# Corner tiles in paired products, high parts on ScalarE, and a copy of the taps for the left and upper tiles

## The reference

```python
def _L0_conv_ref(x, kernel):            # x (128, 55, 55, 96), kernel (96, 5, 5), fp32
    ch = x.shape[-1]
    k = jnp.transpose(kernel, (1, 2, 0))[:, :, None, :]
    y = lax.conv_general_dilated(x, k, window_strides=(1, 1), padding='SAME',
                                 dimension_numbers=('NHWC', 'HWIO', 'NHWC'), feature_group_count=ch)
    return x + y
```

## Time and profile before

| | us |
|---|---|
| three runs | 820.22, 820.39 (median), 821.93 |
| the profiled execution | 820.37 |
| its span, first to last instruction | 818.6 |
| TensorE busy | 805.5 |
| VectorE, ScalarE, GpSimd busy | 690.1, 624.1, 525.6 |

### The profile page before, as it was taken

How to read it: one execution, slowest core, us unless ns; L and a number is a source line. 1 busy time by engine, 2 the same in 40 slices (tenths; PEclk the granted TensorE clock), 3 DMA queues, 4 the chain that set the end, 5 groups by cost and what they waited for, 6 DMA issues and landing times.

```text
span 818.6 us, 19135 instructions
## 1 busy us (share of the span) xinstructions
PE 805.5 (98%) x6912; PEld 805.4 (98%) x6912; DVE 690.1 (84%) x1828; ACT 624.1 (76%) x1442; POOL 525.6 (64%) x652
## 2 busy tenths in 40 slices
PE   5999999999999999999999999999999999999997
PEld 5999999999999999999999999999999999999997
DVE  6898888888888888888888888888888888888885
ACT  5777878787777778787777778787777777787775
POOL 7858566576665675756748566576565674756741
PEclk9999999999999999999999999999999999999999
DMA  9999999999999999999999999999999999999965
GB/s 357 426 426 408 375 381 363 383 368 385 368 370 389 364 381 376 375 381 364 378 377 379 386 368 370 377 376 378 382 361 382 372 386 376 368 376 376 381 261 229
DMA packets 28749, 304.43 MB, mean 372 GB/s; under 512 B 3184, under 2 KB 3312, under 8 KB 4208
## 3 DMA queue, kind: packets, MB, share of 16 engines
q1 hardware_dynamic: 28656, 303.22, 97.1%
HBM read 153.79 MB, written 149.42 MB: 370 GB/s over the span
## 4 chain that ended last, share of the span: by engine, by line
PE 98%; POOL 1%; DMA 0%; issue 0%; DVE 0%; ACT 0%; DVEq 0%
PE sums L380 33%; PE sums L383 33%; PE sums L382 33%; DMA first<-consts 0%; POOL matrix L263 0%; POOL spread L250 0%; POOL spare L238 0%; POOL taps L241 0%; POOL taps L236 0%; DVE y_out L333 0%; ACT y_out L292 0%; DVEq L132 0%
## 5 line engine op out<-in xcount | busy, mean ns | idle before, releaser
L380 PE MATMUL sums<-matrix,x_low 126*128 126x208 f32 (+5 forms) x2304 | 648.1, 281 | 8.3 <-POOL matrix L263 8.3
L383 PE MATMUL sums<-matrix,x_high 126*128 126x208 f32 (+5 forms) x2304 | 647.3, 281 | 0.0
L382 PE MATMUL sums<-matrix,x_high 126*128 126x208 f32 (+5 forms) x2304 | 646.3, 281 | 0.0
L292 ACT ACTIVATE y_out<-sums 128x270 f32<-128x270 f32 (+6 forms) x1152 | 443.4, 392 | 183.3 <-PE sums L383 179.5
L263 POOL TENSOR_TENSOR matrix<-spread,mask 127x300 fp32r<-127x300 f32 x384 | 338.5, 913 | 262.3 <-PE sums L383 262.1
L380 PEld LDWEIGHTS sums<-matrix,x_low 126*128 126x128 f32 (+1 forms) x2304 | 443.9, 193 | 8.2 <-POOL matrix L263 8.2
L383 PEld LDWEIGHTS sums<-matrix,x_high 126*128 126x128 f32 (+1 forms) x2304 | 444.3, 193 | 0.0
L382 PEld LDWEIGHTS sums<-matrix,x_high 126*128 126x128 f32 (+1 forms) x2304 | 444.2, 193 | 0.0
L333 DVE TENSOR_TENSOR y_out<-sums,y_out 128x120 f32<-128x120 f32 (+3 forms) x1344 | 295.5, 255 | 117.7 <-ACT y_out L292 113.8
L323 DVE TENSOR_TENSOR x_low<-x_in,x_high 128x768 fp32r<-128x768 f32 x384 | 379.8, 989 | 2.0 <-ACT x_high L285 2.0
L285 ACT ACTIVATE x_high<-x_in 128x768 fp32r<-128x768 f32 x288 | 239.8, 833 | 6.0 <-DMA x_in<-x 5.8
(11 more groups left out here) (4 smaller groups left out, 0.4 us busy)
## 6 DMA issues: line engine op xcount, KB each, us to landing
x_in<-x SPq DMA_DIRECT2D x95, 1536.0 KB, 9.9
y<-y_out SPq DMA_DIRECT2D x95, 1520.0 KB, 12.9
rest<-later SPq DMA_DIRECT2D x1, 2300.0 KB, 14.4
x_in<-x SPq DMA_DIRECT2D x4, 384.0 KB, 5.5
y<-y_out SPq DMA_DIRECT2D x1, 832.5 KB, 3.4
y<-y_out SPq DMA_DIRECT2D x1, 687.5 KB, 4.0
mask<-masks SPq DMA_DIRECT2D x1, 300.0 KB, 3.7
first<-consts SPq DMA_DIRECT2D x1, 125.0 KB, 2.1
```

What stands on the lines that cost most here:

```text
L292: act.activation(outputs(c, rows, cols), sums(c, t, rows, cols), ACT.Copy).then_inc(copied, 1)
L380: pe.matmul(target, low, turned[HIGH], start=tile is bank["tiles"][0], stop=False, skip_group_check=True)
L382: pe.matmul(target, high, turned[LOW], start=False, stop=False, skip_group_check=True)
L383: product = pe.matmul(target, high, turned[HIGH], start=False, stop=last, skip_group_check=True)
```

## The change

1. **Corner pairs.** In the four corner tiles (tile 0 of quarter 0, the fifth of quarter 1, the last of quarter 2, the second of quarter 3) the two products with `x_high` become one matmul. It streams the low and the high taps' slices, one behind the other (2 x 11 x 16 columns), and writes two places of the bank: the high product where it stood, the low one in 16 extra cells of each row. Banks with a corner so have rows of 46 cells. VectorE adds the low part to `y_out` in an add of its own of 11x16 cells.
2. **High parts.** `cast_high` is gone; ScalarE makes all four quarters' `x_high`, after banks 1, 3, 5 and 7; `x_low` stands after banks 4, 6, 7 and 9 instead of 4, 5, 7 and 9.
3. **Border tiles.** GpSimd copies, after the two parts of each kind's matrix, columns 2 to 17 of 14 of its rows into `edge`, where the 16 cells of a row lie without a gap. The tiles with `from_col` 2 read their taps there. TensorE's wait for a matrix now counts the copy too (`STEPS`).

```diff
+CORNERS = ((0, 0), (2, 0), (2, 1), (0, 1))
+SPAN = 2 * LONG + HALO
+EDGE = LONG + HALO
+EDGE_ROWS = SHORT + 2 * HALO + 1
+STEPS = 3 * KINDS
-HIGH_AFTER = (2, 5, 7)
-CAST_AFTER = 2
-LOW_AFTER = (4, 5, 7, 9)
+HIGH_AFTER = (1, 3, 5, 7)
+LOW_AFTER = (4, 6, 7, 9)
...
+            row, k = CORNERS[quarter]
+            corner = k if n == row else None
...
+                              deep=short[1] - short[0], pitch=SPAN + EDGE * (corner is not None)))
...
+        if bank["corner"] is not None:
+            cells_of_corner = bank["corner_cells"]
+            after = [n + 1 for n, e in enumerate(earlier) if meet(e, cells_of_corner)]
+            bank["adds"].append((cells_of_corner, after[-1] if after else 0, LOW))
+            earlier.append(cells_of_corner)
...
+        edge = [[sbuf(f"edge{i}_{k}", [P, 2, EDGE_ROWS, EDGE], F32R) for k in range(KINDS)] for i in range(SLOTS)]
...
+        def low_sums(c, t):
+            plane = plane_of(c, t)[:, :, SPAN:SPAN + EDGE]
+            return plane.rearrange("p x y -> p y x") if PLAN[t]["kind"] == TALL else plane
+
+        def both_sums(window, wide):
+
+            return bass.AP(tensor=window.tensor, offset=window.offset,
+                           ap=[window.ap[0], [SPAN - wide[0], 2], window.ap[1], window.ap[2]])
...
+                    pool.wait_ge(matrix_step, STEPS * c + 3 * kind + 2)
+                    pool.tensor_copy(
+                        edge[c % SLOTS][kind][0:whole, :, :, :],
+                        matrix[c % SLOTS][kind][0:whole, :, :].bitcast(F32).rearrange("p h (r q) -> p h r q", q=COLS)[
+                            :, :, 0:EDGE_ROWS, HALO:HALO + EDGE]).then_inc(matrix_step, 1)
...
-                dve.tensor_copy(x_high[c % SLOTS][:, cols], x_in[c % X_SLOTS][:, cols]).then_inc(cast_done, 1)
...
-                    dve.tensor_tensor(y, sums(c, t, rows, cols), y, ALU.add).then_inc(added, 1)
+                    terms = sums(c, t, rows, cols) if part == HIGH else low_sums(c, t)
+                    dve.tensor_tensor(y, terms, y, ALU.add).then_inc(added, 1)
...
-                            pe.wait_ge(matrix_step, 2 * KINDS * c + 2 * (kind + 1))
+                            pe.wait_ge(matrix_step, STEPS * c + 3 * (kind + 1))
...
+                        if tile["from_col"]:
+                            turned = edge[c % SLOTS][kind][0:pixels, :, cells, :]
+                        else:
+                            turned = matrix[c % SLOTS][kind][0:pixels, :, :].rearrange("p h (r q) -> p h r q", q=COLS)[
+                                :, :, cells, 0:wide[1] - wide[0]]
...
+                        if bank["corner"] is not None and tile is bank["tiles"][bank["corner"]]:
+                            product = pe.matmul(both_sums(target, wide), high, turned, start=False, stop=last,
+                                                skip_group_check=True)
```

More of the change, by code:

```diff
@@ L79, in banks_of_plane @@
                     from_row=short[0] - (v - HALO), from_col=a - (u - HALO)))
-            banks.append(dict(quarter=quarter, kind=kind, rows=rows, cols=cols, tiles=tiles,
-                              deep=short[1] - short[0], pitch=long[1] - long[0]))
+            row, k = CORNERS[quarter]
+            corner = k if n == row else None
+            banks.append(dict(quarter=quarter, kind=kind, rows=rows, cols=cols, tiles=tiles, corner=corner,
+                              deep=short[1] - short[0], pitch=SPAN + EDGE * (corner is not None)))
+            if corner is not None:
+                across_it = tuple(long[0] + w for w in tiles[corner]["wide"])
+                banks[-1]["corner_cells"] = (rows, across_it) if kind == FLAT else (across_it, cols)
     return banks
@@ L326, in add_seams @@
             def add_seams(c, t):
-                for n, ((rows, cols), after) in enumerate(PLAN[t]["adds"]):
+                for n, ((rows, cols), after, part) in enumerate(PLAN[t]["adds"]):
                     if n == 0:
@@ L375, in _ @@
                         high, low = x_high[c % SLOTS][0:pixels, images], x_low[c % SLOTS][0:pixels, images]
-                        turned = [matrix[c % SLOTS][kind][0:pixels, part, :].rearrange("p (r q) -> p r q", q=COLS)[
-                            :, tile["from_row"]:tile["from_row"] + deep,
-                            tile["from_col"]:tile["from_col"] + wide[1] - wide[0]] for part in (HIGH, LOW)]
+                        cells = slice(tile["from_row"], tile["from_row"] + deep)
+                        if tile["from_col"]:
[3 more added lines that the diff above has]
+                                :, :, cells, 0:wide[1] - wide[0]]
                         last = tile is bank["tiles"][-1]
-                        pe.matmul(target, low, turned[HIGH], start=tile is bank["tiles"][0], stop=False,
+                        pe.matmul(target, low, turned[:, HIGH], start=tile is bank["tiles"][0], stop=False,
                                   skip_group_check=True)
-                        pe.matmul(target, high, turned[LOW], start=False, stop=False, skip_group_check=True)
-                        product = pe.matmul(target, high, turned[HIGH], start=False, stop=last, skip_group_check=True)
+                        if bank["corner"] is not None and tile is bank["tiles"][bank["corner"]]:
+                            product = pe.matmul(both_sums(target, wide), high, turned, start=False, stop=last,
+                                                skip_group_check=True)
+                        else:
+                            pe.matmul(target, high, turned[:, LOW], start=False, stop=False, skip_group_check=True)
+                            product = pe.matmul(target, high, turned[:, HIGH], start=False, stop=last,
+                                                skip_group_check=True)
                     product.then_inc(sums_done, 1)
```

26 lines of the change are left out of this document (6 added, 20 removed).

## The result

The changed kernel takes 839.12 us in the median of four runs (838.68 to 840.10), the kernel before 820.52 beside it: a ratio of 1.0225, with an interval of 1.0207 to 1.0243. It is slower by 2.2 per cent, where 788.7 us were forecast, and lies outside the range of 780 to 806.

What follows compares the result with a forecast made beforehand. The prediction took TensorE to bound the kernel, its matmuls spaced by weight loads or rows. From 820.4 us it took 21.1 for corner pairs and 11.1 for border copies and added 0.5 at the start: 788.7 us, range 780 to 806.

Steps and rivals of the forecast that it cites:

- pairs: TensorE, four corner tiles a channel: one matmul of 0.169 us replaces two of 0.112 each, gaining 21.1 us.
- border copies: TensorE, six left and upper tiles: packed rows of 16 make matmuls faster, 0.116 us a channel, gaining 11.1 us.
- rival 4: Border tiles on TensorE: column offset is not why they are slow; two pairs cost 0.200 us, total 806; chance 0.06.
- GpSimd goes from 526 to 718 us: GpSimd's busy time with 192 new copies at 1.0 us each, in a span of some 787 us.
- near 702 to 710 us: VectorE's busy time after losing 88 us of casts and gaining 100 us of adds, below TensorE's new 780.
- a hold of 0.21 us for each new copy: GpSimd's new copies: held up by VectorE like the spread copies in the median, 560 against 347 ns.
- Rival 3: VectorE becomes late: copies hold x_low, adding 83 us, so VectorE reaches 793 and the kernel some 803; chance 0.06.
- The two new waits of low adds: VectorE: low adds wait for an earlier VectorE add, said to stand behind adds done in order anyway.
- Rival 1: GpSimd becomes the bound: passes TensorE at 1.28 us a copy, the old time at 1.44; chance 0.11.
- Rival 2: DMA holds the pace: a channel's 3.13 MB at 376 GB/s take 8.32 us, total 816; chance 0.07.
- ScalarE: ScalarE's busy time goes from 624 to 704 us by taking the first quarter's high part, 0.83 us a channel.
- The start: TensorE's first matmul, at 8.25 us before, comes 0.5 us later behind a copy; bounds -0.2 and +1.7.

Runs made afterwards that it cites:

- e5_act_edge: e1_reorder with the two border copies of a channel made by ScalarE instead of GpSimd; 786.99 us, ratio 0.9596 to the kernel before.
- e8_act_edge_no_pair: e6_act_edge_plain with the corner pairs undone, leaving of the change the border copies by ScalarE; 809.96 us, ratio 0.9868.
- e2_no_edge: The changed kernel without the border copies, so border tiles read the matrix at column 2 again; 805.89 us, ratio 0.9819.
- e4_reorder_no_edge: e1_reorder without the border copies, so border tiles read the matrix at column 2 again; 805.57 us, ratio 0.9817.
- e9_idle_copy: e5_act_edge with two more copies a channel on GpSimd, into a buffer that nobody reads; 826.72 us, ratio 1.0071.
- e7_half_low: e1_reorder with x_low computed for half of the columns, low parts of half of the tiles left out; 785.86 us, ratio 0.9573.
- e1_reorder: The changed kernel with the low adds of banks 0, 5 and 8 moved behind later seams and the first x_low one bank later; 832.23 us, ratio 1.0140.
- e3_no_pair: The changed kernel without corner pairs, keeping the GpSimd border copies and the high parts on ScalarE; 824.8 us, ratio 1.0052.
- e6_act_edge_plain: The changed kernel with the two border copies of a channel made by ScalarE, VectorE's order left as it is; 802.32 us, ratio 0.9772.

## Why the prediction was wrong

**What bounds the kernel, pairs, border copies: right.** TensorE bounded the kernel before, and its terms come out wherever the other engines let it run. The sum gave 788.7 us and 8.02 a channel; e5_act_edge takes 786.99 and 7.99. The copies alone were to gain 11.1 us less 0.5 at the start, and gain 10.6 (e8_act_edge_no_pair). The prediction's sum has a slip that hardly counts: three times 0.02 is 0.06, not 0.068. The pairs were to gain 21.1 and gain 23.0. Without the copies two of the four pairs read the matrix at column 2, and rival 4 had these at 0.200 instead of 0.169: 820.4 - 21.1 + 2 x 0.031 x 96 = 805.3, and e2_no_edge and e4_reorder_no_edge take 805.9 and 805.6. It shows in the timeline of the weight loads of a pair (L407, L423) and the two behind it, in e4_reorder_no_edge and in e5_act_edge (start us, us): the second and third are 0.20 apart where the pair reads from column 2, 0.16 where it reads the copy.

```profile
301.50 0.19 PEld L407 LDWEIGHTS sums<-matrix,x_high 126*128 126x128 f32 x1
301.61 0.19 PEld L404 LDWEIGHTS sums<-matrix,x_low 126*128 126x128 f32 x1
301.81 0.19 PEld L410 LDWEIGHTS sums<-matrix,x_high 126*128 126x128 f32 x1
```

```profile
300.73 0.19 PEld L423 LDWEIGHTS sums<-edge,x_high 126*128 126x128 f32 x1
300.85 0.19 PEld L420 LDWEIGHTS sums<-matrix,x_low 126*128 126x128 f32 x1
301.01 0.19 PEld L426 LDWEIGHTS sums<-matrix,x_high 126*128 126x128 f32 x1
```

By the median over the 96 channels of e4_reorder_no_edge, 0.31 us lie between the first and the third of these starts at the two corners that read column 2, and 0.28 at the two that read column 0. In e5_act_edge it is 0.28 at all four, and their places in the banks are the same. So the column offset is why those tiles were slow, and rival 4 falls.

**The step that failed: "GpSimd goes from 526 to 718 us ... still with idle time" and VectorE "near 702 to 710 us ... These edits cost nothing as long as that holds".** The copy's own price was about right (0.86 for 1.0). Left out was what the copy, and to a lesser part the new order, does to the instructions that stood there already. GpSimd came to 756: the 526 of before, copies of 165, matrices 66 longer, spread copies 19 longer (125 instead of 106), the splitting of the taps 16 shorter, and overlaps. VectorE came to 795, and the 82 us of `x_low` are nearly all of the miss: without them it stands at 713. Of these 82, 61 go with the copies, and of the matrices' 66, 20 (e2_no_edge). The prediction costed a hold of 0.21 us for each new copy and none for its partner. In the runs it falls on both sides: e9_idle_copy for VectorE by GpSimd's load, e7_half_low for GpSimd by VectorE's.

**Rival 3 had the mechanism and its price (83 us on `x_low`, VectorE at 793), with a chance of 0.06, and a time 36 us too low.** It was set aside because `x_low` stood at a median of 947 against a least of 939. That median was read wrongly as a sign that GpSimd hardly holds it. It says only that less than half were held: 93 of 384 took over 1.0 us, and the mean, 989, and the most, 1579, had already shown what a meeting costs. GpSimd then waited 262 us for TensorE; where the new copies take that waiting away (e9_idle_copy beside e5_act_edge), `x_low`'s median goes from 948 to 1218. That the 83 us came so near is partly luck: they were 0.43 for each of 192 copies, where 384 `x_low` grew by 0.21 each.

An estimate that fits the runs whose chain is GpSimd's or TensorE's: a channel needs on GpSimd, by the least or median durations, four matrices of 0.836, two copies of 0.57, two spreads of 0.356 and some 0.45 for the taps (0.58, 0.62 and 0.61 where nothing meets them, every fourth channel), 5.65 us; and on VectorE four `x_low` of 0.947, 3.79. Together 9.44 if they never overlap, over a channel of 8.0. The runs in which GpSimd sets the pace (e1_reorder, e3_no_pair, e9_idle_copy) go at 8.50, 8.40 and 8.45, about nine tenths of that sum. Without GpSimd's copies the sum is 8.30, with half of `x_low` 7.84; nine tenths of these lie under 8.0, and TensorE sets the pace in both. The factor is fitted, not explained; a part of it is that neighbours on one engine overlap, as the two matrices that take 1.61 and not 1.67 when nothing holds them.

The prediction had quoted the Trainium skill (SBUF — State Buffer, section "SBUF: two separate sides") for a lock that holds a VectorE instruction with two SBUF inputs and a GpSimd one that reads SBUF apart, either way round, and worked it out for the new copies alone. The runs bear the rule out in direction, on both engines; in size only roughly: beside an `x_low` of 0.96 the two matrices at the start were 0.73 late by the median of one matrix, and 0.80 by the 1.61 that two take together when nothing holds them. The same section says that ScalarE never waits there, and the copy on ScalarE agrees, 588 to 682 ns in all 192 of e5_act_edge against 562 to 1397 on GpSimd.

**"The two new waits of low adds ... stand behind adds that are done in order anyway": wrong.** They are in order, but an add that waits for the one before it loses their overlap: in the trace of the change an add that follows another at once and need not wait for it starts some 0.08 us before that one ends (median), and the four of a channel that must wait start 0.03 to 0.10 us after. That is 19 to 22 us of VectorE's busy time (e6_act_edge_plain against e5_act_edge, e2_no_edge against e4_reorder_no_edge, the change against e1_reorder). There are also three such new places in a channel and not two: the first seam add now waits for the low add of bank 0. The last step from rival 3's 803 to 839 lies in part in such losses: the page has 30.8 us of idle time before the adds, of which only 4.3 end with ScalarE; in e1_reorder it is 46.0 of 47.9. The adds in turn free the banks and `y_out` slots for which TensorE and ScalarE wait. How much of the 36 us is each was not parted, and with the waits gone GpSimd still holds the kernel at 832 (e1_reorder): rival 3 had left out that `x_low` holds GpSimd too.

**Rival 1** (GpSimd the bound) is what e1_reorder and e3_no_pair become, though with copies at 0.95 us, far under the 1.44 that it asked for: again because the matrices grew. **Rival 2** (DMA) falls as the bound: e5_act_edge moves 392 GB/s, as the forecast wanted. **ScalarE** was costed too high (704, measured 666). **The start**: the first matmul comes at 9.55, +1.3 instead of +0.5, inside its bounds.

## What to carry to other kernels

Work put on an engine with idle time can be paid for by work that stood there already, on that engine and on another. Before giving GpSimd a copy, add up the unheld time of GpSimd and of VectorE's instructions with two inputs in SBUF over one period. Here copies on GpSimd cost time where the sum was 9.44 us for a period of 8.0, and at 8.30, with the copies on ScalarE, they did not. A median near the least says only that less than half of the instructions were held, not that meeting is cheap; look at the mean and the most, and ask what kept the rest apart. And place an add that needs the result of another some instructions behind it.

## What the runs showed of the hardware

- VectorE's `x_low` (two SBUF inputs, 768 columns) and GpSimd's matrices slow each other from 0.94 and 0.82 us to as much as 1.64 and 1.65, while the seam adds, which have one input in PSUM, keep their 276 ns at 120 values beside a GpSimd that is 90 per cent busy.
- With half of `x_low` gone, the same GpSimd program needs 591 us instead of 785.
- The same 1728 adds keep VectorE busy for 19 to 22 us longer where some wait for the add just before them than in the same kernel with none that does: 394.8 against 373.3, 395.4 against 376.7, 400.6 against 381.4 us. In the changed kernel an add that need not wait starts some 0.08 us before the end of the one in front of it, one that must wait 0.03 to 0.10 after.
- A matmul of 22 rows of 16 fp32r columns read from column 2 of rows of 20 holds up the next by 0.03 us more than one read from column 0 (0.31 against 0.28 us to the second weight load behind it).
